# The last layers' second map with tokens on partitions, added to x in one step, and a written-out start of the attention

## The reference, cut to what matters

```
x = x + 0.5 * ffn(layernorm(x))          # first feed-forward block
x = x + attention(layernorm(x))          # 16 heads, softmax over 512 keys
x = x + 0.5 * ffn(layernorm(x))          # second feed-forward block, same weights

def ffn(h):                              # three layers, D = 128
    for blk in range(3):
        y = linear(h, 2*blk)             # first map: dequantised weights, LoRA, bias
        y = gelu(layernorm(y) * gamma + beta)
        h = linear(y, 2*blk + 1) + h     # second map, plus the state h
    return h
```

## Time and profile before

| What | Value |
|---|---|
| median of three runs | 1004.29 us |
| the profiled execution's own time | 1005.08 us |
| its span, first to last instruction | 1003.3 us |
| mean granted TensorE clock, share of full | 0.986 |
| PE busy | 961.0 us, 96% |
| DVE busy | 863.7 us, 86% |
| POOL busy | 832.4 us, 83% |
| ACT busy | 809.2 us, 81% |

### The profile page before, as it was taken

How to read it: one execution, slowest core, us unless ns; L and a number is a source line. 1 busy time by engine, 2 the same in 40 slices (tenths; PEclk the granted TensorE clock), 3 DMA queues, 4 the chain that set the end, 5 groups by cost and what they waited for, 6 DMA issues and landing times.

```text
span 1003.3 us, 19251 instructions
## 1 busy us (share of the span) xinstructions
PE 961.0 (96%) x5892; PEld 501.5 (50%) x5892; DVE 863.7 (86%) x1754; ACT 809.2 (81%) x1343; POOL 832.4 (83%) x940
## 2 busy tenths in 40 slices
PE   5888699999999999999999999999999999999897
PEld 4674244444444444444444444444444444445675
DVE  7677789999999999999999999999999988995566
ACT  3875489888888888888888888888888888888673
POOL 2654588889998999899989999999999998899452
PEclk9998799999999999999999999999999999999999
DMA  9000312233323333333333333333233232330002
GB/s 249 1 2 12 83 40 61 62 64 64 64 62 64 64 64 64 64 64 64 64 64 64 64 63 65 64 64 63 57 65 63 60 64 62 63 63 14 2 1 84
DMA packets 71743, 59.88 MB, mean 60 GB/s; under 512 B 11168, under 2 KB 70560, under 8 KB 71648
## 3 DMA queue, kind: packets, MB, share of 16 engines
q1 hardware_dynamic: 71392, 58.31, 26.8%
q10 hardware_dynamic: 256, 0.39, 0.2%
HBM read 6.23 MB, written 2.10 MB: 8 GB/s over the span
## 4 chain that ended last, share of the span: by engine, by line
PE 90%; DVE 5%; POOL 2%; issue 1%; ACT 1%; DMA 1%; SPq 0%; DVEq 0%; POOLq 0%; ACTq 0%
PE ps L1162 12%; PE ps L1163 11%; PE ps L1154 11%; PE ps L1164 11%; PE ps L1155 11%; PE ps L1147 7%; PE ps L1092 3%; PE ps L1139 3%; PE ps L1181 3%; PE ps L1177 3%; PE ps L1178 3%; PE ps L1064 3%; PE ps L1140 3%; PE ps L1141 3%; PE ps L1074 1%; PE ps L1031 1%
## 5 line engine op out<-in xcount | busy, mean ns | idle before, releaser
L468 POOL TENSOR_TENSOR p_lo<-work_b,p_hi 128x1024 f16<-128x1024 f32 x256 | 540.2, 2132 | 45.9 <-ACT p_hi L620 45.1
L907 DVE TENSOR_REDUCE mcol<-ps 128x2 f16<-128x1024 f32 x256 | 301.1, 1220 | 5.0 <-PE ps L1147 4.8
L615 ACT ACTIVATE work_b<-ps,exp_scale 128x1024 f32<-128x1024 f32 x256 | 271.6, 1111 | 35.2 <-PE ps L1155 35.2
L620 ACT ACTIVATE p_hi<-work_b 128x1024 f16<-128x1024 f32 x256 | 256.1, 1055 | 0.0
L1162 PE MATMUL ps<-p_hi,xn_hi 128*128 128x512 f16 x512 | 195.4, 382 | 3.8 <-POOL p_lo L468 3.8
L1154 PE MATMUL ps<-head_ops 128*128 128x512 f16 x512 | 195.0, 381 | 1.3 <-DVE mcol L907 1.3
L1155 PE MATMUL ps<-head_ops 128*128 128x512 f16 x512 | 195.1, 381 | 0.0
L1163 PE MATMUL ps<-p_hi,xn_lo 128*128 128x512 f16 x512 | 194.8, 380 | 0.0
L1164 PE MATMUL ps<-p_lo,xn_hi 128*128 128x512 f16 x512 | 194.6, 380 | 0.0
L477 POOL TENSOR_TENSOR x<-x,o_sb 128x512 f32<-128x512 f32 x128 | 163.1, 1274 | 7.2 <-DVE o_sb L935 2.1
L918 DVE STREAM_TRANSPOSE head_ops<-mcol 32x128 f16<-32x128 f16 x512 | 155.4, 304 | 9.3
(11 more groups left out here) (132 smaller groups left out, 1376.5 us busy)
## 6 DMA issues: line engine op xcount, KB each, us to landing
head_ops<-pair_ops SPq DMA_DIRECT2D x512, 64.0 KB, 2.0
head_ops<-pair_ops SPq DMA_DIRECT2D x128, 128.0 KB, 2.4
x<-x_dram SPq DMA_DIRECT2D x8, 256.0 KB, 5.8
out<-x SPq DMA_DIRECT2D x8, 256.0 KB, 2.6
vo_last<-wvo_dram SPq DMA_DIRECT2D x1, 1024.0 KB, 12.3
qk<-wq_dram SPq DMA_DIRECT2D x1, 512.0 KB, 5.4
qk<-wk_dram SPq DMA_DIRECT2D x1, 512.0 KB, 6.2
scl<-scales_dram ACTq DMA_DIRECT2D x8, 48.0 KB, 5.5
```

What stands on the lines that cost most here:

```text
L468: pool.tensor_tensor(p_lo[:, k % 2, rows, :], p32[:, k % 2, rows, :], p_hi[:, k % 2, rows, :], ALU.subtract).then_inc(plo_done, 1)
L615: nc.scalar.activation(p32[:, k % 2, 2 * a:2 * a + 2, :], s_ps[a], ACT.Exp, scale=exp_scale[:, 0:1]).then_inc(exp_done, 1)
L620: nc.scalar.activation(p_hi[:, k % 2, 2 * a:2 * a + 2, :], p32[:, k % 2, 2 * a:2 * a + 2, :], ACT.Copy).then_inc(phi_done, 1)
L907: nc.vector.tensor_reduce(mcol[:, pair % 2, :, t, 0], s_ps[t % 2], AX.X, ALU.max, negate=True).then_inc(max_red, 1)
```

## The change

The second map of the third layer is made with tokens on partitions. Per batch PE transposes the state into the batch's bank, adds the bias by a fourth row of `bias_rows`, and adds four products with the activations as the stationary operand. DVE then adds half of the bank to x. `post`, `h_tile`, `step_x_half` and the semaphore `post_t` are gone.

```diff
-            def lin2(f, i):
+            def lin2(f, i, batches=(0, 1)):
                 n = i // UNITS
-                for c, b in unit_batches(i):
+                for c, b in [unit_batches(i)[c] for c in batches]:
                     pe.wait_ge(gl_ready, at(f, i, c))
-                    nc.tensor.matmul(bank[f][b], wt[:, 2 * n + 1, :], work_a[:, b, :], start=True,
-                                     stop=True).then_inc(lin2_done, 1)
+                    if n < NB - 1:
+                        nc.tensor.matmul(bank[f][b], wt[:, 2 * n + 1, :], work_a[:, b, :], start=True,
+                                         stop=True).then_inc(lin2_done, 1)
+                        continue
+                    for t in range(TT):
+                        cols = slice(t * 128, (t + 1) * 128)
+                        nc.tensor.matmul(bank[f][b][:, cols], hT[:, b, cols], ident[:, :], is_transpose=True,
+                                         start=(t == 0), stop=False)
+                    row = bias_rows[:, NB, :].rearrange("p (a d) -> p a d", a=1).to_broadcast([128, TT, D])
+                    nc.tensor.matmul(bank[f][b].rearrange("p (t d) -> p t d", d=D), ones_b[:, :], row,
+                                     start=False, stop=False)
+                    for t in range(TT):
+                        cols = slice(t * 128, (t + 1) * 128)
+                        ins = nc.tensor.matmul(bank[f][b][:, cols], work_a[:, b, cols], wt[:, 2 * n + 1, :],
+                                               start=False, stop=(t == TT - 1))
+                    ins.then_inc(lin2_done, 1)
...
+            def step_x(f, i, c):
+                b = 2 * (i % UNITS) + c
+                dve.wait_ge(lin2_done, at(f, i, c))
                 rows = x[:, b * TT:(b + 1) * TT, :].rearrange("p a d -> p (a d)")
+                nc.vector.scalar_tensor_tensor(rows, bank[f][b], 0.5, rows, ALU.mult, ALU.add).then_inc(x1_ready, 1)
```

The slots -6 to 0 are replaced by a written-out order on PE, ACT and DVE; the loop starts with slot 1. The maxima of pair 1 go to banks 6 and 7 instead of banks 0 to 3 (`max_ps`). The order on PE at the seam:

```diff
             lin2(0, STEPS - 3)
             turn_z(0, STEPS - 2)
+            lin2(0, STEPS - 2, [0])
             for h in range(2):
                 wait_attn_xhat(pe, 0, h)
+                turn_half(half_of(bank[0][0], h), x_tile(0), h, xn_t)
+            lin2(0, STEPS - 2, [1])
...
+            project_k(0)
+            project_q(0)
+            turn_z(0, STEPS - 1)
+            pair_ready(0)
+            for t in range(2):
+                pe.wait_ge(x1_ready, 4 + 2 * t)
+                maxima(0, t)
+            project_k(1)
+            lin2(0, STEPS - 1, [0])
+            pe.wait_ge(max_red, 1)
+            maxima(0, 2)
+            project_q(1)
+            pe.wait_ge(max_red, 2)
+            maxima(0, 3)
+            lin2(0, STEPS - 1, [1])
+            head_ready(0)
+            for a in range(2):
+                scores(0, 0, a)
+            pair_ready(1)
+            pe.wait_ge(x1_ready, B)
+            maxima(1, 0)
+            head_ready(1)
+            for a in range(2):
+                pe.wait_ge(exp_done, 1 + a)
+                scores(1, 1, a)
+            pe.wait_ge(max_red, 5)
+            maxima(1, 1)
+            project_k(2)
+            pe.wait_ge(ql_ready, 2)
+            pe.wait_ge(xnl_ready, 2)
+            pe.wait_ge(plo_done, 1)
+            weigh(0, 0)
+            pe.wait_ge(max_red, 6)
+            maxima(1, 2)
+            weigh(0, 1)
+            project_q(2)
+            pe.wait_ge(max_red, 7)
+            maxima(1, 3)
+            pe.wait_ge(plo_done, 2)
+            weigh(0, 2)
+            weigh(0, 3)
+            pair_ready(2)
+            for a in range(2):
+                pe.wait_ge(exp_done, 3 + a)
+                maxima(2, a)
+            project_k(3)
```

DVE's order at the seam, and ACT's:

```diff
+            (DVE, in step 11:) step_x(0, 8, 0); seed(0, 11); norm_stats(batch 0); z_scaled(0, 10)
             norm_means, norm_sigmas, norm_apply(half 0)
+            step_x(0, 8, 1); z_scaled(0, 11); split(0, h) for h in 0, 1
+            step_x(0, 9, 0); step_x(0, 9, 1); step_x(0, 10, 0); step_x(0, 10, 1)
+            k_low(0, 0); q_low(0, 0); reduce_max(0, t) for t in 0..3; row_max(0)
+            step_x(0, 11, 0); step_x(0, 11, 1); row_max(1)
+            reduce_max(1, 0); k_low(1, 1); reduce_max(1, 1); q_low(1, 1); reduce_max(1, 2)
+            k_low(2, 0); reduce_max(1, 3); row_max(2); q_low(2, 0)
+            reduce_max(2, 0); reduce_max(2, 1); y_low(0); k_low(3, 1)
...
+            (ACT:) k_high(0, 0); q_high(0, 0); gelu(0, 11); k_high(1, 1); halves_tokens(0, 0 and 1)
+            q_high(1, 1); activation(exp_warm, ident[:, 0:1], ACT.Exp)
+            exps(0, a); p_high(0, a); k_high(2, 0); exps(1, a); q_high(2, 0); p_high(1, a)
+            k_high(3, 1); y_high(0)
```

More of the change, by code:

```diff
@@ L231, in attn_slots @@
             if n == 1:
[L232 to L236, removed]
+                return {"stats": two(1), "means": [2], "newton": [3, 3, 4, 4, 5, 5], "apply": two(6),
+                        "halves": two(8), "turn": two(8), "low": two(12)}
+            k = 16 * n - 19
+            return {"stats": two(k), "means": [k + 2], "newton": list(range(k + 3, k + 9)), "apply": two(k + 9),
+                    "halves": two(k + 11), "turn": two(k + 11), "low": two(k + 15)}
         def ffn_slots(m):
@@ L667, in slot @@
                 late(k)
-                if k >= 0:
-                    if k >= 1:
-                        act.wait_ge(o_done, k)
-                    y_high(k)
-            for k in range(-6, NH - 1):
-                slot(k)
-                if k == -5:
-                    gelu(0, STEPS - 1)
-                if k == -4:
-                    halves_tokens(0, 0)
-                    halves_tokens(0, 1)
+                act.wait_ge(o_done, k)
+                y_high(k)
+            k_high(0, 0)
+            q_high(0, 0)
+            gelu(0, STEPS - 1)
+            k_high(1, 1)
+            halves_tokens(0, 0)
+            halves_tokens(0, 1)
+            q_high(1, 1)
+            nc.scalar.activation(exp_warm[:, :], ident[:, 0:1], ACT.Exp)
+            for a in range(2):
+                exps(0, a)
+            for a in range(2):
+                p_high(0, a)
+            pair_free(2, 0)
+            k_high(2, 0)
+            for a in range(2):
+                exps(1, a)
+            q_high(2, 0)
+            for a in range(2):
+                p_high(1, a)
+            pair_free(3, 1)
+            k_high(3, 1)
+            y_high(0)
+            for k in range(1, NH - 1):
+                slot(k)
             act.wait_ge(plo_done, 2 * (NH - 1))
@@ L978, in slot @@
                         q_low(pair, buf)
+            k_low(0, 0)
+            q_low(0, 0)
+            for t in range(TT):
+                reduce_max(0, t)
+            row_max(0)
+            step_x(0, STEPS - 1, 0)
+            step_x(0, STEPS - 1, 1)
+            row_max(1)
+            reduce_max(1, 0)
+            k_low(1, 1)
+            reduce_max(1, 1)
+            q_low(1, 1)
+            reduce_max(1, 2)
+            pair_free(2, 0)
+            k_low(2, 0)
+            reduce_max(1, 3)
+            row_max(2)
+            q_low(2, 0)
+            reduce_max(2, 0)
+            reduce_max(2, 1)
+            y_low(0)
+            pair_free(3, 1)
+            k_low(3, 1)
             for k in SLOTS:
                 slot(k)
-                if k == -6:
-                    step_h(0, STEPS - 2, 0)
-                    step_h(0, STEPS - 2, 1)
-                if k == -4:
-                    step_h(0, STEPS - 1, 0)
-                    step_h(0, STEPS - 1, 1)
             z_scaled(1, 0)
@@ L998, in _ @@
             for i in range(3, STEPS + 3):
-                step_h(1, i - 3, 0)
-                step_h(1, i - 3, 1)
+                for c in range(2):
+                    if i - 3 < STEPS - UNITS:
+                        step_h(1, i - 3, c)
+                    else:
+                        step_x(1, i - 3, c)
                 if i < STEPS:
@@ L1047, in turn_bias @@
                 pe.wait_ge(prep_a, 1)
-                for n in range(NB):
+                for n in range(NB + 1):
                     ins = nc.tensor.matmul(brow_ps[:, n * D:(n + 1) * D], bias_parts[:, n, :], ident_b[:, :],
```

218 lines of the change are left out of this document (92 added, 126 removed).

## The result

The changed kernel takes 995.38 us in the median of 4 runs (993.64 to 995.85), against 1004.39 (1001.17 to 1006.95, 4 runs). The ratio on record is 0.9901, with a 95% interval of 0.9878 to 0.9923 (it isn't the quotient of the two medians, which is 0.991). So it is faster by 1.0%. The forecast was 997.0, range 991.5 to 1001.5.

What follows compares the result with a forecast made beforehand. PE was taken as the bound among the heads (busy 961 of 1003 us). Terms -9.4 + 2.5 - 2.6 + 0.4 + 1.7 + 0.1 = -7.3 us gave 997.8 from the profiled execution, 997.0 by the median; range 991.5 to 1001.5.

Steps and rivals of the forecast that it cites:

- Seam, first part: Feed-forward to attention, from lin2(8) at 80.0 to first scores: these start at 102.2 instead of 108.93, gain 6.7 us.
- Seam, second part: First scores to head 3's: head 2's scores at 117.4 instead of 126.95, slot 1 6.5 us; 9.4 us gained by head 3.
- The clock: At the seam, one or two stretches of some 5 us at the lower clock level were expected: +2.5 us.
- Rival 2: Clock doesn't fall at the seam at all, or the order packs better than written: 994.5 us; chance 0.15.
- Heads: Among the heads, batches 2 to 7 lose their post turns, 12 halves at 0.22 us each: -2.6 us.
- the term of +0.4: POOL in slots 3 to 5: batch 1's norm iterations add 4.8 us of work; +0.4 us, ends 0 and 2.5.
- The end: Last layer's end: last step_x at 1001.1 instead of 999.4, 1.7 us later; ends +0.5 and +2.5.
- with the same output DMA behind: At the program's end, output DMA behind the last step_x was taken as the same as before.

Runs made afterwards that it cites:

- Experiment 6: Changed kernel with batch 0's layer norm late on DVE and no second map between the turn of step 10 and the xhat turns: 1001.68 us, ratio 0.9964.
- experiment 5: Changed kernel with q_low of pair 1 ahead of pair 1's second reduction on DVE, and k_low of pair 2 ahead of the third: 993.99 us, ratio 0.9895.
- Experiment 1: Kernel before with batch 1's late-norm iterations moved off POOL's first heads (apply, halves and turn to later slots too): 998.63 us, ratio 0.9941.
- experiment 9: Kernel of experiments 8 and 10 with row_max(2) ahead of q_low(2) again on DVE: 990.32 us, ratio 0.9861.
- Experiment 2: Changed kernel with the old end of the second block (turn of h, 512-column products, steps on x behind a turn): 994.73 us, ratio 0.9904.
- experiment 3: Changed kernel with the second batch's product of the last steps put behind the next turn: 994.01 us, ratio 0.9901.
- experiments 8 and 10: One kernel run twice: changed kernel with edits of experiments 3 and 5, turns' waits filled at the seam, q_low(2) ahead of row_max(2): 991.51 and 992.02 us.
- kernels 8 and 9: The kernel of experiments 8 and 10 (991.51 and 992.02 us) and that of experiment 9 (990.32 us).

## Why the prediction was right, and where it wasn't

**Seam, first part: right.** The prediction has the first scores 22.2 us behind the start of lin2(8), and they come 22.33 behind it. Every step of it is in the trace: lin2 at 1.54 us a batch, xhat turns without a wait, four reductions in a row. The waits behind the turns show as 0.43 us and not as 0.59 only because the trace counts from the end of the turn's last record. From the turn's start to lin2 it is 1.47 us (974.29 to 975.76), and I had 1.46. Experiment 6 shows the cause: take the early norm away and the whole part goes (29.1 us to the first scores, where before needs 28.9). That the maxima of pair 1 no longer share banks with the scores, which I had named beside it, was not taken back in a run.

**Seam, second part: right in size, and DVE's queue was the right cause** (head 2's scores 15.5 us behind the first ones, forecast 15.2; slot 1 6.48, forecast 6.5). I had put the chain through POOL's p_low at 108.7. POOL did deliver there (108.87, half of 4.21 us behind 106.76), but the weighing at 109.30 waited for DVE's q_low of pair 1, and experiment 5 takes 1.6 us off by DVE's order alone. Experiment 1 shows what I left open: how much can be had without the new order. Moving POOL's iterations alone gives 5.9 us between the first scores and head 3, and a ratio of 0.9941 against the changed kernel's 0.9901.

**The clock: the step that failed.** "I take +2.5" was to cover one or two stretches at the lower level. There was none: 1.00 in all windows from 80 to 140 in the changed kernel, also where PE had 2.02 us of 4 to do. Rival 2's condition came true, and the median, 995.38, lies nearer to its 994.5 than to the forecast's 997.0. I had argued from before's rows, in which I put the low stretches down to the idle times of 3.64, 1.32 and 3.78 us. For the middle one that reading is wrong. Its matmuls are long from 105.73 on, 3.2 us before the scores that waited 1.32, and the idle times ahead of it are 0.62, 0.79 and 0.65 (before 103.10, 104.33 and 105.37):

```profile
105.73 0.61 PE L1139 MATMUL ps<-xt_hi,w_hi 128*128 128x512 f16 x1
```

The changed kernel has idle times of up to 1.40 us and held full clock. In experiment 9 it fell with 1.40. So neither before's rows nor these give a price for the term; what decides stays open.

The Trainium skill ("TensorE: Matmul & The Clock Gate", "What's actually happening") says that the array is throttled by default and that activity releases it. That gaps are paid twice was my conclusion from it. It holds for the long idle times: experiment 6 has 0.51 behind 4.77 us. For the changed kernel's gaps of up to 1.40 us it doesn't (1.00 throughout).

**Heads: right**, -2.57 against -2.6. **POOL: the term of +0.4 was 0.** The extra work came as reckoned (4.7 us, forecast 4.8), but its lead over PE absorbed it.

**The end: +1.96 against +1.7**, within its bounds of 0.5 and 2.5. Of the missing 0.3, 0.2 is that the batch behind each wait takes 1.60 us (975.76 to 977.36) and not 1.54. What failed is "with the same output DMA behind". Before, the last four batches' steps came as one row of DVE and four transfers left together; now the steps come in pairs 4.6 us apart, 1.5 us apart within a pair, and the drain is 1.1 us shorter. Behind the last step the DMA engines still moved 0.36 MB (128 GB/s over 2.78 us), or 1.4 transfers, where before it was 0.82 MB (211 GB/s over 3.89 us), or 3.1. Experiment 2 brings both back together (15.86 and 3.83). So the end costs 0.9 us net, and experiment 3 takes the cost away while it keeps the short drain.

**The transition: not in the prediction**, and as far as the profiles show not the change's, as six profiles of kernels built on the changed one lose the clock there as before's does. Its idle time of 2.45 us is in every profile here; behind it the four records of lin2 take 1.98 us in four of twelve and 2.6 to 3.7 in eight. That is 1.1 us of the profiled difference, and one reason why the profiles differ by 11.5 and the medians by 9.0.

**The sum.** Forecast -7.3. With the clock's term at 0, POOL's at 0 and the drain's -1.1 it would have been -11.3, and with the seam and the end as measured -10.4. The medians give -9.0. The 1.4 us between may lie in the lower mean clock of the changed kernel's runs that have no profile (0.995 to 0.997), but they are also within the scatter of four runs, so this isn't shown.

That 997.0 came within 1.6 us of 995.38 is in part luck. In the two profiles the difference is 4.2 us larger than the forecast's. The clock (2.5), POOL (0.4), the drain (1.1) and the transition (1.1) were all missed in the same direction, and only the seam (0.7) and the end (0.3) went the other way. The medians hide most of that, as the profiled run of the changed kernel was its quickest.

## What to carry over

Ask of a large reordering which single queue it relieves, and price that alone first: here one table of slots on POOL gave 0.6% by itself, where the whole change gave 1.0%, and the written-out order without the early norm gave less than the table. Where a step gives up an overlap (the GELU behind its own turn), look for another batch's product to lay into it; that took the end's cost away without a trade. And count what is behind the last step too: results that come one by one let the transfers drain behind them.

## What was not expected of the hardware

- The same idle time of 2.45 us on PE is followed by a lower clock in eight of twelve profiled executions and by none in four, with the same instructions around it. These are eleven kernels; the one profiled twice (experiments 8 and 10) lost the clock there both times. The four runs of the changed kernel had mean clocks of 0.995 to 1.000, so the clock does differ between executions of one kernel.
- At the seam the clock held with PE busy for 2.02 of 4 us and gaps of up to 1.40, and fell in three of three profiles of kernels 8 and 9, one of which has the same gaps. Before, it fell behind gaps of 0.62 to 0.79. A gap's length alone doesn't tell.
- A table load of ACT runs ahead of the wait of the activation that needs it (100.15 against 103.57).
- Where four 256 KB outputs leave together the span ends 3.8 to 3.9 us behind the last step (three profiles), where they leave spread 2.7 to 2.8 (nine).
